# A projection as undivided float32 products instead of three float32r products

## The chip, the core and the metric

The kernel runs on one core of one Trainium2 chip. The metric is the device time of an execution in microseconds (us); the median of three runs is compared. The engines are TensorE (PE in the profile, its loads of the stationary operand PEld), ScalarE (ACT), VectorE (DVE), GpSimd (POOL) and SyncE (SP), which issues the DMAs.

## What is computed

A tower of one block over 64 images of 64 patches with 192 features, in three parts: a token mixer, an attention layer with a memory that is updated token by token, and a feed-forward layer. The change touches the projection of the second part. There, for a normalised row `xn` (192 features) and each of k, q and v:

```python
def _modifier(x, w1, b1, w2, b2):
    h = jax.nn.gelu(x @ w1.T + b1, approximate=False)
    return h @ w2.T + b2
...
k = xn @ Wk.T + 0.1 * _modifier(xn, km_w1, km_b1, km_w2, km_b2)
v = xn @ Wv.T + 0.1 * _modifier(xn, vm_w1, vm_b1, vm_w2, vm_b2)
q = xn @ Wq.T + 0.1 * _modifier(xn, qm_w1, qm_b1, qm_w2, qm_b2)
k = _ln(k.reshape(b, s, H, HD), lnk_g, lnk_b)
...
```

with 12 heads (H) of 64 (HD). All inputs are float32.

## The kernel before

Every engine has its own list of instructions, written out in order in one block (`@block.tensor` and so on); they meet through semaphores (`wait_ge`, `then_inc`, and `need`, which waits where a count is positive). So the order on an engine is the order of the code, and an instruction that waits holds up all behind it on its engine.

**First stage, to 422 us.** A short chain first multiplies the five matrices w0 to w4 into one. Then a pipeline runs over 32 pairs of patches: SP loads three weight matrices and the inputs of a pair (`load_pair`, lines 323 to 334, two buffers), TensorE forms q, k, v and p1 products in chunks (lines 485 to 567), and between the chunks of pair n it does the small products of pairs n-1 (transposes at line 519, scores) and n-2. DVE works in the same steps (line 1242); its line 1262 copies the transposed q and k, its line 1276 forms the sum that TensorE transposes at line 537. The result goes to a scratch tensor in device memory.

**The projection's weights** are prepared within this stage. SP loads them at lines 351 to 357, after it has waited for `bt_copied`, since the tile `cw` lies over the buffer `chain_w[1]` of the matrix chain. `cw` has two slots of 128 partitions and 2304 columns (k, q, v): slot 0 for features 0 to 127, slot 1 (113 rows used, AUG) for features 128 to 191, the 48 hidden values of the modifier and its bias. DVE takes the mean over each head's 64 columns off (`centre_weights`) and splits the result into `cw_hi`, a float32r tile, and `cw_lo`, the rest (`split_weights`). These four blocks follow DVE's own work in steps 2, 3, 4 and 5 (`step_b_and_weights`, line 1302).

**Second stage, from 440 us.** GpSimd fills constants (lines 1084 to 1089), then 32 tiles of 128 rows pass through a pipeline; in step s five to six tiles are in work, tile x = s at the input, t = s - 1 at the projection, j, k, l, m behind. TensorE's list of a step is at lines 789 to 833: it opens with 64x64 products (line 708) and the 12 transposes of `turn_kq` (line 657, 32 times in all, once per tile), and the six pieces of the projection (`project`) lie between other work in the order 1; 3, 0; 2; 4, 5. `PIECES` (line 58) holds their columns, widths (512, 256, 256, 512, 512, 256) and which of k, q, v they belong to. Each piece is the sum over the two slots of `xr_hi*cw_hi + xr_hi*cw_lo + xr_lo*cw_hi`.

The projection's input `x_aug` (four columns of 128: the first 128 features, and three versions of the rest with the GELU values of k, q, v below) is written by ACT (`copy_x`, `gelu`), in one buffer. ACT copies it to `xr_hi` (`high_part`, line 992) and DVE forms `xr_lo` (`low_part`, line 1495), both in two buffers; TensorE waits for `xr_ready` before piece 1 (line 622).

A product is one call of `mm` (line 442) in the code. In the trace a product of float32 operands is two pairs of LDWEIGHTS and MATMUL, one of float32r operands is one pair.

Of the kernel before, what the change touches and what calls it, by code (L numbers as in the profile page):

```python
# [18 lines left out]
F32R = mybir.dt.float32r  # L19
# [48 lines left out]
 mod_mm mod_ready gate_mm gate_ready xr_hi xr_ready  # L68
# [39 lines left out]
def build(nc, d, out):  # L108

    with ExitStack() as ctx:  # L110
# [42 lines left out]
        gate_b = sb("gate_b", [R2 + 1, ATT])  # L153
# [6 lines left out]
        cw_hi = sb("cw_hi", [P, 2, ALL], F32R)  # L160
        cw_lo = sb("cw_lo", [P, 2, ALL], F32R)

# [59 lines left out]
        cw = chain_w[1].rearrange("p a b -> p (a b)").rearrange("p (k n) -> p k n", k=2)  # L222
# [11 lines left out]
        x_aug = part("second", P, 4, P)  # L234
        xg1 = part("second", P, P)
        xg2 = part("second", R2 + 1, P)
# [37 lines left out]
        xr_hi, xr_lo = [[sb(f"{name}{i}", [P, 4, P], F32R) for i in range(2)] for name in ("xr_hi", "xr_lo")]  # L274
# [20 lines left out]
        def _(sp):  # L295
# [55 lines left out]
            sp.wait_ge(S["bt_copied"], 2)  # L351
            settled(sp)
            for dst, src in [(cw[:, 0, :], d["kqvT"][0:P]), (cw[0:R2, 1, :], d["kqvT"][P:ATT]),
                             (cw[R2:AUG, 1, :], d["modT"]), (mod1a[:, :], d["mod1T"][0:P]), (mod1b[:, :], d["mod1T"][P:2 * P]),
                             (gate_a[:, :], d["gateT"][0:P]), (gate_b[:, :], d["gateT"][P:ATT + 1]), (wo[:, :, :], d["WoT"]),
# [85 lines left out]
        def _(pe):  # L441
# [136 lines left out]
            pe.wait_ge(S["cw_ready"], 2)  # L578
# [19 lines left out]
            def modifier(x):  # L598
# [3 lines left out]
                for part, w in enumerate((mod1a, mod1b)):  # L602
                    for i in range(2):
                        last = nc.tensor.matmul(PS[0:MOD_PAIR, 7, i * P:(i + 1) * P], w[:, i * MOD_PAIR:(i + 1) * MOD_PAIR],
                                                x_aug[:, part, :], start=part == 0 and i == 0, stop=part == 1,
                                                skip_group_check=True)
# [231 lines left out]
        def _(act):  # L838
# [50 lines left out]
            act.wait_ge(S["region_ready"], 6)  # L889
# [742 lines left out]
```

## Time and profile before

| | us |
|---|---|
| median of three runs | 1265.63 |
| the three runs | 1265.08, 1265.63, 1268.97 |
| the profiled execution | 1262.91 |
| its span | 1260.7 |
| TensorE busy | 1169.6 (93%), 18596 matmuls |
| loads of the stationary operand busy | 954.3 (76%) |
| DVE, ACT, GpSimd busy | 786.3, 722.8, 560.7 |
| HBM read, written | 154.87 MB, 22.02 MB |

The span is from the first to the last instruction, and the execution's time is 2.2 us more. TensorE's ends are modelled and its instructions overlap, so its busy time says when it had something in work, not how fast it went: the distance between starts tells that.

### The profile page before, as it was taken

Reading aid. Unit: us, or ns where it says so; the run is one execution under the profiler, and the core shown is the slowest. Engines: PE = TensorE matmul, PEld = TensorE weight load, DVE = VectorE, ACT = ScalarE, POOL = GpSimd, SP = SyncE. Lnnn points to the kernel's source line nnn. Section 1 sums busy time; section 2 is a strip of 40 time slices with the busy share of each in tenths; the row PEclk is TensorE's granted clock in tenths of the full one; section 3 lists DMA queues with packets and bytes.
Section 4 is the critical chain, followed back from the end, with each engine's and each line's share of the span. In section 5 each row is a group of like instructions: output and inputs, shape, how many; then the busy total and the mean of one; then the engine's idle time right before and its main releaser. Section 6 shows DMA issues by size and latency. Waiting matters only on the chain.

```text
span 1260.7 us, 47618 instructions
## 1 busy us (share of the span) xinstructions
PE 1169.6 (93%) x18596; PEld 954.3 (76%) x18596; DVE 786.3 (62%) x2152; ACT 722.8 (57%) x1955; POOL 560.7 (44%) x690
## 2 busy tenths in 40 slices
PE   5899999999999558999999999999999999999975
PEld 5865666666666356888888888888888888888864
DVE  0027433333333335787888888887887887888862
ACT  0012222222222247788888888888888888888752
POOL 0000000000000046676776676776676776676631
PEclk8999999999999778999999999999999999999997
DMA  9979999999998001212222222222222222222220
GB/s 320 341 279 352 360 373 375 375 382 372 374 369 330 16 13 25 50 36 41 49 45 39 49 47 39 49 47 41 47 46 39 49 47 40 48 48 36 45 43 21
DMA packets 220196, 179.54 MB, mean 142 GB/s; under 512 B 164406, under 2 KB 190073, under 8 KB 219513
## 3 DMA queue, kind: packets, MB, share of 16 engines
q1 hardware_dynamic: 220010, 176.94, 45.2%
q8 instruction: 131, 2.15, 0.7%
q14 instruction: 55, 0.45, 0.1%
HBM read 154.87 MB, written 22.02 MB: 140 GB/s over the span
## 4 chain that ended last, share of the span: by engine, by line
POOL 36%; PE 31%; issue 23%; DVE 6%; SPq 2%; DMA 1%; ACT 1%; POOLq 0%; DVEq 0%; ACTq 0%
PE PS L443 28%; POOL region L1148 15%; POOL region L1131 6%; POOL region L1136 3%; POOL region L1142 2%; POOL region L1114 1%; POOL region L1098 1%; POOL region L1121 1%; POOL region L1107 1%; DVE region L1454 1%; PE PS L519 1%; SPq L312 1%; POOL region L1111 1%; POOL region L1100 1%; PE PS L537 1%
## 5 line engine op out<-in xcount | busy, mean ns | idle before, releaser
L443 PE MATMUL PS<-region 64*64 64x64 f32 (+6 forms) x5864 | 349.9, 284 | 20.7 <-DVE region L1196 12.2
L443 PEld LDWEIGHTS PS<-region 64*64 64x64 f32 (+3 forms) x5864 | 228.4, 137 | 120.4 <-issue 107.0
L1148 POOL TENSOR_TENSOR region<-region,powers 128x12 f32<-128x12 f32 x96 | 237.2, 2471 | 7.6 <-POOL region L1142 0.2
L1077 POOL TENSOR_TENSOR region<-region,powers 128x1 f32<-128x1 f32 x32 | 6.1, 189 | 404.0 <-DVE region L1256 404.0
L708 PE MATMUL PS<-region 64*64 64x64 f32 x4608 | 154.4, 220 | 2.3 <-ACT region L959 2.1
L708 PEld LDWEIGHTS PS<-region 64*64 64x64 f32 x4608 | 144.4, 134 | 14.9 <-issue 9.2
L443 PE MATMUL PS<-cw_hi,xr_hi 128*128 128x256 f32 (+3 forms) x384 | 145.5, 379 | 3.8 <-DVE xr_lo L1495 1.2
L926 ACT ACTIVATE region<-PS 128x512 f32<-128x512 f32 (+1 forms) x192 | 93.7, 489 | 77.6 <-PE PS L443 74.4
L443 PE MATMUL PS<-cw_lo,xr_hi 128*128 128x256 f32 (+3 forms) x384 | 130.6, 340 | 0.0
L443 PE MATMUL PS<-cw_hi,xr_lo 128*128 128x256 f32 (+3 forms) x384 | 130.4, 340 | 0.0
L849 ACT ACTIVATE region<-PS 128x384 f32<-128x384 f32 x32 | 15.7, 491 | 192.7 <-PE PS L443 192.7
L1131 POOL TENSOR_TENSOR region<-region,powers 128x12 f32<-128x12 f32 x32 | 74.8, 2337 | 107.5 <-DVE region L1448 107.5
L1378 DVE TENSOR_REDUCE region<-region 128x12 f32<-128x768 f32 x96 | 90.2, 943 | 10.5 <-ACT region L931 10.5
L999 ACT ACTIVATE region<-region 128x64 f32<-128x64 f32 x384 | 94.8, 335 | 0.0
L443 PEld LDWEIGHTS PS<-cw_hi,xr_hi 128*128 128x128 f32 (+1 forms) x384 | 73.7, 192 | 16.9 <-ACT region L938 1.8
L906 ACT ACTIVATE region<-PS,vecs 128x256 f32<-128x256 f32 (+1 forms) x128 | 75.9, 670 | 14.0 <-PE PS L657 13.8
L931 ACT ACTIVATE region<-region 128x768 f32<-128x768 f32 x96 | 80.1, 838 | 1.0
L443 PEld LDWEIGHTS PS<-cw_hi,xr_lo 128*128 128x128 f32 (+1 forms) x384 | 73.3, 191 | 8.8
L443 PEld LDWEIGHTS PS<-cw_lo,xr_hi 128*128 128x128 f32 (+1 forms) x384 | 74.5, 194 | 7.1
L443 PE MATMUL PS<-p1w,region 128*128 128x192 f32 x384 | 74.4, 335 | 0.0
L443 PE MATMUL PS<-wo,region 128*128 128x192 f32 x384 | 71.0, 335 | 2.0 <-ACT region L895 2.0
L698 PE MATMUL PS<-region 64*64 64x64 f32 x3072 | 61.3, 226 | 11.3 <-issue 8.4
(171 smaller groups left out, 2184.6 us busy)
## 6 DMA issues: line engine op xcount, KB each, us to landing
region<-in_Wq SPq DMA_DIRECT2D x32, 1152.0 KB, 5.9
region<-in_Wk SPq DMA_DIRECT2D x32, 1152.0 KB, 8.2
region<-in_Wv SPq DMA_DIRECT2D x32, 1152.0 KB, 8.0
region<-in_x SPq DMA_DIRECT2D x32, 384.0 KB, 6.9
n_scratch<-region SPq DMA_DIRECT2D x64, 192.0 KB, 3.5
region<-h_scratch SPq DMA_DIRECT2D x64, 96.0 KB, 3.1
region<-in_w SPq DMA_DIRECT2D x2, 2304.0 KB, 13.4
region<-i_scratch SPq DMA_DIRECT2D x256, 12.0 KB, 1.8
```

What stands on the lines that cost most here:

```text
L443: return nc.tensor.matmul(dst, lhsT, rhs, start=first, stop=last)
L698: done = nc.tensor.matmul(dst(slice(to, to + 64), h), lhsT[rows, h, :], rhs(rows, h), start=h < 2, stop=stop, skip_group_check=True)
L708: done = nc.tensor.matmul(dst(rows, h), eT[rows, h, :], rhs(rows, h), start=start and h == odd, stop=stop, skip_group_check=True)
L906: act.activation(kqT[:, pairs, m, :], PS[:, bank, at:at + n * P].rearrange("p (a b) -> p a b", a=n), ACT.Identity, scale=(lnk_g, lnq_g)[m] ...
L926: act.activation(raw[:, col:col + width], PS[:, PIECE_BANK[i], 0:width], ACT.Copy).then_inc(S["raw_ready"], 1)
L931: act.activation(sq[:, m * KD:(m + 1) * KD], raw[:, m * KD:(m + 1) * KD], ACT.Square, scale=HD ** -0.5).then_inc(S["sq_ready"], 1)
L999: last = act.activation(vs[j % 2][:, h * HD:(h + 1) * HD], raw[:, 2 * KD + h * HD:2 * KD + (h + 1) * HD], ACT.Copy, scale=rs[:, 2 * HEADS ...
L1131: pool.tensor_tensor(norm[:, 1, :], norm[:, 0, :], square_root[:, 0:HEADS], ALU.pow).then_inc(S["n1"], 1)
L1136: pool.tensor_tensor(nscale[:, :, :], mask_n.unsqueeze(1).to_broadcast([P, HEADS, SEQ]), norm[:, 5, :].unsqueeze(2).to_broadcast([P, HEADS ...
L1142: pool.tensor_tensor(rs_var[:, cols], ssq[:, cols], eps[:, cols], ALU.add).then_inc(S["rs_var"], 1)
L1148: pool.tensor_tensor(rs[:, cols], rs_var[:, cols], root[:, cols], ALU.pow).then_inc(S["rs_ready"], 1)
L1378: dve.tensor_reduce(ssq[:, m * HEADS:(m + 1) * HEADS], sq.rearrange("p (g d) -> p g d", d=HD) [:, m * HEADS:(m + 1) * HEADS, :], AX, ALU.a ...
```

## The change

The projection's products take the float32 operands as they are. What goes: the float32r tiles `cw_hi`, `cw_lo`, `xr_hi`, `xr_lo`; the split of the weights on DVE; `high_part` on ACT and `low_part` on DVE; their signals. What comes: `x_aug` in two buffers of its own, written and read by the parity of the tile; `cw` as a tile of its own, so that SP's loads no longer wait for `bt_copied`; rows up to 128 in the second slot of `cw`, in `gate_b` and in `xg2`, zero in the weights; the centring in six blocks, one for each slot and each of k, q, v, in the steps 2 to 7; the memset of the two `x_aug` before GpSimd's wait for the end of the first stage.

```diff
-        cw_hi = sb("cw_hi", [P, 2, ALL], F32R)
-        cw_lo = sb("cw_lo", [P, 2, ALL], F32R)
+        cw = sb("cw", [P, 2, ALL])
...
-        xr_hi, xr_lo = [[sb(f"{name}{i}", [P, 4, P], F32R) for i in range(2)] for name in ("xr_hi", "xr_lo")]
+        x_aug = [sb(f"x_aug{i}", [P, 4, P]) for i in range(2)]
...
             load_pair(Step(0, 1))
-            sp.wait_ge(S["bt_copied"], 2)
-            settled(sp)
             for dst, src in [(cw[:, 0, :], d["kqvT"][0:P]), (cw[0:R2, 1, :], d["kqvT"][P:ATT]),
-                             (cw[R2:AUG, 1, :], d["modT"]), (mod1a[:, :], d["mod1T"][0:P]), (mod1b[:, :], d["mod1T"][P:2 * P]),
+                             (cw[R2:P, 1, :], d["modT"]), (mod1a[:, :], d["mod1T"][0:P]), (mod1b[:, :], d["mod1T"][P:2 * P]),
...
-            pe.wait_ge(S["cw_ready"], 2)
+            pe.wait_ge(S["cw_ready"], 6)
...
                     if i == 1:
-                        pe.wait_ge(S["xr_ready"], t + 1)
                         pe.wait_ge(S["mod_ready"], 3 * t + 3)
...
                     dst = PS[:, PIECE_BANK[i], 0:width]
-                    n = 0
-                    for k, parts in ((0, P), (1, AUG)):
-                        for xs, ws in ((xr_hi[t % 2], cw_hi), (xr_hi[t % 2], cw_lo), (xr_lo[t % 2], cw_hi)):
-                            slot = 0 if k == 0 else 1 + m
-                            last = mm(dst, xs[0:parts, slot, :], ws[0:parts, k, col:col + width], n == 0, n == 5)
-                            n += 1
-                    last.then_inc(S["piece_mm"], 1)
+                    mm(dst, x_aug[t % 2][:, 0, :], cw[:, 0, col:col + width], True, False)
+                    mm(dst, x_aug[t % 2][:, 1 + m, :], cw[:, 1, col:col + width], False, True).then_inc(S["piece_mm"], 1)
...
             def copy_x(x):
                 act.wait_ge(S["xT_mm"], x + 1)
-                need(act, "xr_ready", x)
+                need(act, "piece_mm", 6 * (x - 1))
+                need(act, "mod_mm", x - 1)
                 need(act, "gate_mm", x)
...
+            for buf in x_aug:
+                pool.memset(buf[:, :, :], 1.0).then_inc(S["region_ready"], 1)
             pool.wait_ge(S["h_out0"], PAIRS // 2 * 32)
             pool.wait_ge(S["h_out1"], PAIRS // 2 * 32)
-            for i, (dst, value) in enumerate(((x_aug, 1.0), (xg2, 1.0), (y2T2, 0.0), (dT, 0.0), (inv, 0.0))):
+            for i, (dst, value) in enumerate(((xg2, 1.0), (y2T2, 0.0), (dT, 0.0), (inv, 0.0))):
...
-            dve.wait_ge(S["region_ready"], 5)
+            dve.wait_ge(S["region_ready"], 7)
...
-                if s.known and 2 <= s.n < 6:
-                    (centre_weights, split_weights)[s.n % 2]((s.n - 2) // 2)
+                if s.known and 2 <= s.n < 8:
+                    centre_weights(s.n - 2)
```

The new `centre_weights` of one block:

```python
def centre_weights(part):

    k, m = divmod(part, 3)
    group = cw[:, k, m * KD:(m + 1) * KD].rearrange("p (g d) -> p g d", d=HD)
    mine = slice(m * HEADS, (m + 1) * HEADS)
    if part == 0:
        dve.wait_ge(S["cw_in"], 160)
        dve.tensor_scalar(cw[R2:P, 1, :], cw[R2:P, 1, :], 0.1, None, ALU.mult).then_inc(S["cw_step"], 1)
    ...
```

On TensorE, around piece 2 of a tile in the second stage, between the output projection (`wo`) and the transposes of the next input, there stood before (a row is a product of the program, x6 six in a row; the width is that of the moving operand):

```order
L443 MATMUL PS<-wo,region 128x192 x6
L443 MATMUL PS<-cw_hi,xr_hi 128x256
L443 MATMUL PS<-cw_lo,xr_hi 128x256
L443 MATMUL PS<-cw_hi,xr_lo 128x256
L443 MATMUL PS<-cw_hi,xr_hi 128x256
L443 MATMUL PS<-cw_lo,xr_hi 128x256
L443 MATMUL PS<-cw_hi,xr_lo 128x256
L594 MATMUL PS<-cst,region 128x128
```

and now:

```order
L437 MATMUL PS<-wo,region 128x192 x6
L437 MATMUL PS<-cw,x_aug 128x256 x2
L588 MATMUL PS<-cst,region 128x128
L589 MATMUL PS<-cst,region 64x128
L588 MATMUL PS<-cst,region 128x128
```

Six products of a piece became two; what stands before and behind is the same.

On DVE, in step 2 of the first stage, between the step's last instruction (the scaling of its result) and the first of step 3, there stood before:

```order
L1300 TENSOR_SCALAR region<-region 128x192
L1224 TENSOR_SCALAR region<-region 49x2304
L1226 TENSOR_REDUCE cw_sum<-region 128x36
L1228 TENSOR_SCALAR cw_mean<-cw_sum 128x36
L1230 TENSOR_TENSOR region<-region,cw_mean 128x2304
L1250 SCALAR_TENSOR_TENSOR region<-PS,region 128x192
```

and now:

```order
L1275 TENSOR_SCALAR region<-region 128x192
L1208 TENSOR_SCALAR cw<-cw 64x2304
L1210 TENSOR_REDUCE cw_sum<-cw 128x12
L1212 TENSOR_SCALAR cw_mean<-cw_sum 128x12
L1214 TENSOR_TENSOR cw<-cw,cw_mean 128x768
L1225 SCALAR_TENSOR_TENSOR region<-PS,region 128x192
```

The block now covers a third of a slot's columns; the other blocks follow in the steps behind it.

## Rows read from the trace of the kernel before

In a timeline and in the chain a row gives the start and the length in us, the engine, the line, what was done, and, in square brackets, how long the engine stood idle before it and what ended that. In the busy time by stretch a row gives the stretch, its length, for each of PE, PEld, DVE, ACT and POOL the busy us and in brackets the instructions, then TensorE's granted clock (1.00 is full speed), the DMA engines' share and GB/s. The list of waits gives us in total, how often, and the longest. A group row gives its count, then busy us, mean ns of one, and idle us before.

**Rows 1.** Busy time of the engines in three stretches of the run.

```profile
60.00:420.00 360.00, 353.49 (x2586) 226.85 (x2585) 147.32 (x445) 89.73 (x337) 22.14 (x60) 1.00 0.93 347
...
441.00:516.00 75.00, 53.35 (x688) 45.96 (x688) 39.77 (x99) 44.49 (x105) 41.43 (x51) 0.82 0.14 26
516.00:1179.00 663.00, 656.23 (x13782) 585.37 (x13779) 542.56 (x1449) 546.48 (x1399) 468.31 (x529) 1.00 0.24 44
```

**Rows 2.** Timeline of TensorE: line 657 at five steps of the second stage.

```profile
471.40 2.38 PE L657 MATMUL PS<-cst,region 128*128 128x128 f32 x12 [4.24 <-DVE wo L1317]
...
491.78 2.82 PE L657 MATMUL PS<-cst,region 128*128 128x128 f32 x12 [4.60 <-DVE region L1384]
...
516.13 1.53 PE L657 MATMUL PS<-cst,region 128*128 128x128 f32 x12
...
1178.90 1.72 PE L657 MATMUL PS<-cst,region 128*128 128x128 f32 x12
...
1202.29 1.53 PE L657 MATMUL PS<-cst,region 128*128 128x128 f32 x12
```

**Rows 3.** TensorE's list of waits, 460 to 1240 us, one entry.

```profile
PE PS L698 <- issue: 8.4, 30, 1.2
```

**Rows 4.** Timeline of TensorE, one full step.

```profile
877.76 2.22 PE L443 MATMUL PS<-wo,region 128*128 128x192 f32 x12
...
882.62 0.50 PE L443 MATMUL PS<-cw_hi,xr_hi 128*128 128x512 f32 x1
882.96 0.39 PE L443 MATMUL PS<-cw_lo,xr_hi 128*128 128x512 f32 x1
...
884.13 0.28 PE L443 MATMUL PS<-cw_hi,xr_hi 128*128 128x256 f32 x1
...
884.84 0.60 PE L604 MATMUL PS<-region,mod1a 128*112 128x128 f32 x4
```

**Rows 5.** Timeline of TensorE, first stage, a run of 384-wide products.

```profile
75.66 1.51 PE L443 MATMUL PS<-region 128*64 128x384 f32 x8
```

**Rows 6.** Timelines of TensorE (line 519) and DVE (the weights), first stage.

```profile
97.73 0.64 PE L519 MATMUL PS<-cst,region 128*96 128x128 f32 x4
...
111.77 0.64 PE L519 MATMUL PS<-cst,region 128*96 128x128 f32 x4
...
122.95 0.64 PE L519 MATMUL PS<-cst,region 128*96 128x128 f32 x4
...
135.47 0.64 PE L519 MATMUL PS<-cst,region 128*96 128x128 f32 x4
...
168.78 0.64 PE L519 MATMUL PS<-cst,region 128*96 128x128 f32 x4
...
94.37 1.36 DVE L1224 TENSOR_SCALAR region<-region 49x2304 f32<-49x2304 f32 x1
...
98.56 2.56 DVE L1230 TENSOR_TENSOR region<-region,cw_mean 128x2304 f32<-128x2304 f32 x1
...
109.67 2.56 DVE L1239 TENSOR_TENSOR cw_lo<-region,cw_hi 128x2304 fp32r<-128x2304 f32 x1
```

**Rows 7.** Chain that ended last, in order of time, 436 to 454 us.

```profile
440.31 0.54 POOL region L1087
...
451.87 0.64 ACT xr_hi L992
452.53 0.70 DVE xr_lo L1495
```

**Rows 8.** Timelines of GpSimd and DVE, second tile step.

```profile
466.18 2.27 POOL L1148 TENSOR_TENSOR region<-region,powers 128x12 f32<-128x12 f32 x1
...
467.89 1.83 DVE L1384 TENSOR_TENSOR region<-region 128x768 f32<-128x768 f32 x2
```

**Rows 9.** Groups of weight loads by form: busy us, mean ns of one.

```profile
L443 PEld LDWEIGHTS PS<-cw_hi,xr_lo 128*128 128x128 f32 x192 | 36.7, 191 | 4.5
```

**Rows 10.** Part 4 of the page: chain that ended last, by engine.

```profile
POOL 36%; PE 31%; issue 23%; DVE 6%; SPq 2%; DMA 1%; ACT 1%; POOLq 0%; DVEq 0%; ACTq 0%
```

More of the change, by code:

```diff
@@ L18 @@
 F32 = mybir.dt.float32
-F32R = mybir.dt.float32r
 ALU = mybir.AluOpType
@@ L233, in build @@
         xh = part("second", P, ATT)
-        x_aug = part("second", P, 4, P)
         xg1 = part("second", P, P)
-        xg2 = part("second", R2 + 1, P)
+        xg2 = part("second", P, P)
         gate = [part("second", P, ATT) for _ in range(4)]
@@ L604, in modifier @@
                         last = nc.tensor.matmul(PS[0:MOD_PAIR, 7, i * P:(i + 1) * P], w[:, i * MOD_PAIR:(i + 1) * MOD_PAIR],
-                                                x_aug[:, part, :], start=part == 0 and i == 0, stop=part == 1,
+                                                x_aug[x % 2][:, part, :], start=part == 0 and i == 0, stop=part == 1,
                                                 skip_group_check=True)
@@ L887, in _ @@
             pipeline(act, PAIRS, 2, step_b)
-            act.wait_ge(S["region_ready"], 6)
+            act.wait_ge(S["region_ready"], 7)
             def turned_out(l):
@@ L946, in gelu @@
                 for m, (at, i) in enumerate(((slice(0, MOD), 0), (rows, 0), (rows, 1))):
-                    act.activation(x_aug[rows, 1 + m, :], PS[at, 7, i * P:(i + 1) * P], ACT.Gelu,
+                    act.activation(x_aug[x % 2][rows, 1 + m, :], PS[at, 7, i * P:(i + 1) * P], ACT.Gelu,
                                    bias=mod_bias[at, i:i + 1]).then_inc(S["mod_ready"], 1)
@@ L985, in relu @@
                 act.activation(f1[:, :], PS[:, 6, 2 * P:3 * P], ACT.Relu, bias=ffn_b1).then_inc(S["f1_ready"], 1)
-            def high_part(x):
-                act.wait_ge(S["mod_ready"], 3 * x + 3)
-                act.wait_ge(S["xlin_copied"], 2 * x + 2)
-                need(act, "piece_mm", 6 * (x - 1))
-                need(act, "xr_ready", x - 1)
-                act.activation(xr_hi[x % 2][:, :, :], x_aug[:, :, :], ACT.Copy).then_inc(S["xr_hi"], 1)
             def scale_v(j):
@@ L1233, in split_weights @@
[L1233 to L1240 removed]
+            def centre_weights(part):
[3 more added lines that the diff above has]
+                if part == 0:
+                    dve.wait_ge(S["cw_in"], 160)
+                    dve.tensor_scalar(cw[R2:P, 1, :], cw[R2:P, 1, :], 0.1, None, ALU.mult).then_inc(S["cw_step"], 1)
+                dve.wait_ge(S["cw_step"], 2 * part + 1)
+                dve.tensor_reduce(cw_sum[:, k, mine], group, AX, ALU.add).then_inc(S["cw_step"], 1)
+                dve.wait_ge(S["cw_step"], 2 * part + 2)
+                dve.tensor_scalar(cw_mean[:, k, mine], cw_sum[:, k, mine], 1.0 / HD, None, ALU.mult).then_inc(S["cw_step"], 1)
+                dve.wait_ge(S["cw_step"], 2 * part + 3)
+                dve.tensor_tensor(group, group, cw_mean[:, k, mine].unsqueeze(2).to_broadcast([P, HEADS, HD]),
+                                  ALU.subtract).then_inc(S["cw_ready"], 1)
@@ L1490, in normalise @@
                 dve.tensor_scalar(xh[:, :], xn[:, :], rstd_parts[:, 5:6], None, ALU.mult).then_inc(S["xh_ready"], 1)
-            def low_part(x):
-                dve.wait_ge(S["xr_hi"], x + 1)
-                need(dve, "piece_mm", 6 * (x - 1))
-                dve.tensor_tensor(xr_lo[x % 2][:, :, :], x_aug[:, :, :], xr_hi[x % 2][:, :, :].bitcast(F32), ALU.subtract).then_inc(S["xr_ready"], 1)
             def ffn_out(l):
@@ L1597, in host_layout @@
     d["mod1T"] = tall(np.concatenate([k1, gap(R2 - MOD), q1, gap(R2), v1], axis=1))
-    d["modT"] = np.concatenate([np.concatenate([a[f"attn_{m}m_w2"].T, row(a[f"attn_{m}m_b2"])]) for m in "kqv"], axis=1)
+    below = np.zeros((P - AUG, KD), np.float32)
+    d["modT"] = np.concatenate([np.concatenate([a[f"attn_{m}m_w2"].T, row(a[f"attn_{m}m_b2"]), below]) for m in "kqv"], axis=1)
     d["kqvT"] = np.concatenate([a["attn_Wk"].T, a["attn_Wq"].T, a["attn_Wv"].T], axis=1)
-    d["gateT"] = np.concatenate([a["attn_Wg"].T, row(a["attn_bg"])])
+    d["gateT"] = np.concatenate([a["attn_Wg"].T, row(a["attn_bg"]), np.zeros((2 * P - ATT - 1, ATT), np.float32)])
     d["WoT"] = a["attn_Wo"].T.reshape(HEADS // 2, P, ATT).transpose(1, 0, 2)
```

35 lines of the change are left out of this document (6 added, 29 removed).

## The prediction

> **What bounds the kernel now.** I read the stretches first. From 516 to 1179 us, the stage of the 32 tiles once it is full, TensorE is busy 656.23 of 663 us, DVE 542.56, ACT 546.48, GpSimd 468.31, and the DMA engines a quarter of their time [rows 1]. A busy PE proves little by itself, so the start times come next. The transposes of line 657 open each step. From the one at 516.13 to the one at 1178.90 there are 28 steps, (1178.90 - 516.13) / 28 = 23.67 us each [rows 2]. In that stage the longest entry in TensorE's list of waits is 8.4 us over 30 waits, 0.28 us a step, before line 698, where a chain through DVE has a fixed length [rows 3]. So TensorE works through its list almost without a gap: a microsecond more in its list is a microsecond more in the step. The stage of the 32 pairs before it is the same kind: PE 353.49 of 360 us busy, while the DMA engines stand at 0.93 [rows 1]; its steps, read from the transposes of line 519, are (168.78 - 135.47) / 3 = 11.10 us [rows 6].
>
> **Part 1, the projection's products.** Per tile there are six pieces, three 512 wide and three 256 wide, each with two contraction slots. Before, a slot is three float32r products of one instruction each: 36 instructions. Start to start, five of them at 512 take 884.13 - 882.96 = 1.17 us, 0.234 each; six at 256 take 884.84 - 884.13 = 0.71 us, 0.118 each [rows 4]. That is 18 x 0.234 + 18 x 0.118 = 6.34 us a tile.
> After, a slot is one float32 product, and every float32 product of this kernel is two instructions. No row shows one with 512 columns, so I bound it. The output projection (wo, 192 columns) has 12 instructions in 2.22 us [rows 4]; less the length of the last one (0.33) and what the first one takes extra (0.10), (2.22 - 0.33 - 0.10) / 11 = 0.163 us from start to start, that is 2 x 192 columns at 2.4 GHz (0.160) and 2.5 ns. At 384 columns eight instructions, running two by two on the halves of the array, last 1.51 us, of which the first has some 0.05 extra and the last 0.49 is its own length: (1.51 - 0.49 - 0.05) / 3 = 0.323 a pair [rows 5], again 2 x 384 / 2.4 and 2.5 ns. By this line an instruction at 512 takes 0.429 us and one at 256 takes 0.216. Twelve of each: 5.15 + 2.59 = 7.74 us a tile. In passes: six before, eight after. The first-instruction delay after a group of 64x64 products is 0.34 - 0.23 = 0.11 us for float32r [rows 4] and about 0.10 for float32 at wo, so that cancels.
> Difference: **+1.40 us a tile**. From below the bound is the pure column count, 12 x 0.427 + 12 x 0.213 = 7.68, +1.34. From above: a float32r instruction at 512 takes 0.234 where its columns need 0.213, 9% more; if wide float32 products had the same excess, 7.68 x 1.09 = 8.4, +2.05. I take the line through 192 and 384, since both points are float32 and the excess does not show at either.
> The Trainium skill, FP8 and Floating Point Precision, section Matmul Precision, says that true FP32 is four passes through the array; the 0.163 us for half of a 192-column product agrees, and it adds nothing to the sum.
> Over the 28 full steps: 28 x 1.40 = **+39.2 us**. Nothing hides it, because the neighbours on TensorE are already back to back.
>
> **Part 2, the split of the input.** ACT loses line 992 (0.63 us a tile), DVE loses line 1495 (0.69) [rows 7]. In full steps neither engine is the bound, and the cover is TensorE's own list: worth 0. Once, at the first tile, both lie on the chain of waits: GELU ends at 451.87, then 0.64 and 0.70, then the first piece. After, the first piece follows the GELU: **-1.3 us** [rows 7]. At the second tile the same pair stands before line 1384 on DVE, but its second product also needs GpSimd's power (started 466.18, 2.27 us long, so 468.45), while DVE began the two products at 467.89 (0.9 each); the wait that takes over gives back all but 0.3 [rows 8].
>
> **Part 3, the start of the tile stage.** GpSimd's memset of x_aug, 0.54 us, leaves the chain between the stages; DVE now waits also for the last small memset, about 0.17: **-0.4 us**, if the load of h has landed by then; from 0 to -0.5 [rows 7]. Tiles 0 to 2 run in steps with real waits of TensorE (4.24 before 471.40, 4.60 before 491.78 [rows 2]) and partly at half clock (granted 0.82 over 441 to 516 us [rows 1]). Three tiles at 1.40 are 4.2, half clock adds about 0.5; against it stand the 0.3 of part 2 twice, and waits late in the third step that the longer pieces fill. I take **+2.4**, bounds 0 to 6. The last tile's step (1178.90 to 1202.29 [rows 2], already shorter than a full one) is taken at **+1.2**.
>
> **Part 4, the weights in the first stage.** DVE centres and splits the weights between its pair steps, in four blocks: a scaling and a centring of 6.75 us (94.37 to 98.56 + 2.56), a split of 3.9 (a conversion as long as the scaling, 1.36, and the subtraction of 2.56 that ends at 112.23), and both again for the second slot without the scaling [rows 6]. DVE stands in order, so the block holds up its line 1262 and 1276 of the next step and TensorE behind them. The price is in the steps: 97.73, 111.77, 122.95, 135.47, that is 14.04, 11.18 and 12.52 us where 11.10 is normal, 4.4 us too long together; the 3.9 us block cost 0.1 [rows 6]. After, there are six blocks, one in each of six steps. A reduction and a subtraction over a third of the columns take a third of 2.56 and some 0.1 fixed, 0.95 each, and the small scaling between them 0.2: 2.1 us, the first with 1.36 more, 3.5. All lie under 3.9, so **-4.3 us**; from -4.6 to -2, should loads set the pace when TensorE stops waiting (0.93 of the DMA time is used).
> The ten weight loads on SP no longer wait for bt_copied, and are issued some 12 us earlier. They stand behind the loads of pair 1 in a stretch where the DMA engines are full, and pair 2 waits for TensorE to leave its buffer: 0.
>
> **The sum.** 39.2 + 1.2 + 2.4 - 1.3 - 0.4 - 4.3 = +36.8 us. On the profiled execution's 1262.91 that gives 1299.7. That execution lies 2.7 below the median of the three timed ones, 1265.63; the same difference on the median gives **1302 us**.
>
> **Rivals.**
> *Wide float32 products carry the 9% excess*: 2.05 instead of 1.40 a tile, 31 tiles x 0.65 = +20: 1322. Against: none at 192 or 384 columns. 7%.
> *The weight blocks still hold up DVE*, or loads then set the pace: the 4.3 us do not come back, 1306. 7%.
> *Faster, by weight loads.* Were TensorE paced by its loads of the stationary operand, the count would decide: 36 loads a tile before, 24 after. Place: the pieces of all 32 tiles; price: 12 loads at the 0.11 us at which 128-column transposes follow each other, 1.3 us x 32 = -42, and -6 of parts 2 to 4: 1218. It decides only where a product streams for less than its load takes. For: loads are busy 585.37 of 663 us [rows 1]. Against: loads of 0.19 us at 256 columns follow at 0.118, at 512 columns at 0.234 [rows 4, 9]: the pace goes with the columns streamed. 2%. The Trainium skill, Perfetto Trace Analysis, section Identifying the Most-Contended Engine, says to judge by the busy share of LDWEIGHTS, not of matmuls; by that rule the change would help, and the start times here speak against it.
> *Faster, by the freed engines.* If a loop through ACT and DVE set the 23.67 us, with TensorE only filling it, the step would fall by the 0.63 of line 992 until TensorE's list is longer than the loop: about -20 and -6, which gives 1240. For: the chain that ended last goes through GpSimd for 36% and TensorE for only 31% [rows 10]. Against: TensorE has no gap that another engine ends [rows 3]. 4%.
> *No change*: the eight passes hide in waits that these views do not show, 1263. 3%.
>
> **Chances and range.** The forecast's own case (1302, parts 1 to 4 with their bounds: 1294 to 1310) holds 77%. About 0.3%, 4 us, is what a measurement of this kernel tells from no change. Faster by more 6%, within 3%, slower by more 91%. The range for 8 in 10 takes in the case without part 4 and part of the excess: 1289 to 1318.
>
> **What would show it.** Right: full steps of 25.1 us between the transposes that open them; 512-wide float32 instructions following at 0.43 and 256-wide at 0.22; line 519's steps all near 11.1 from 97 us on; the first piece 0.1 us after the GELU. Wrong: steps at 23.7 or below; wide instructions at 0.47; a new wait of TensorE for ACT or DVE in full steps; first-stage steps that still read 12 to 14 us.

## The result, and the profile after

Timed beside the kernel before on the same chip, the changed kernel takes **1301.16 us** (median of 4 runs, 1299.39 to 1301.68) against 1265.36 (1264.27 to 1268.97). The ratio is 1.0275, with a 95% interval of 1.0253 to 1.0298: slower, by 35.8 us. The profiled execution has a span of 1299.5 us; that of the kernel before, from which the rows ahead of the prediction come, has 1260.7.

First the busy time by stretch in the changed kernel, with the columns of [rows 1].

```profile
60.00:420.00 360.00, 356.89 (x2600) 229.85 (x2598) 142.49 (x456) 90.20 (x339) 22.13 (x60) 1.00 0.93 348
506.00:1200.00 694.00, 687.06 (x13285) 545.57 (x13281) 520.41 (x1402) 522.59 (x1344) 450.75 (x521) 1.00 0.23 42
```

TensorE is as full as before in both stages, with fewer instructions in the second (13285 in 694 us for 13782 in 663) and about as many in the first (2600 for 2586); DVE and ACT have become a little emptier, since the split is gone and the step is longer. Next the transposes that open a full step (line 657 before, line 645 now), which answer to [rows 2].

```profile
512.40 1.53 PE L645 MATMUL PS<-cst,region 128*128 128x128 f32 x12
...
1215.65 1.53 PE L645 MATMUL PS<-cst,region 128*128 128x128 f32 x12
1239.76 1.53 PE L645 MATMUL PS<-cst,region 128*128 128x128 f32 x12
```

The 28 steps take (1215.65 - 512.40) / 28 = 25.12 us each; before it was 23.67. Most steps of after are 25.05 us and most of before 23.63, a difference of 1.42. The first full step opens 3.7 us earlier than before (512.40 for 516.13). So the loss is made between these two marks, nearly all of it as a fixed price for each step.

What TensorE does in one of these steps, from its timeline, which answers to [rows 4]:

```profile
901.55 2.85 PE L437 MATMUL PS<-cw,x_aug 128*128 128x512 f32 x8
904.24 0.60 PE L598 MATMUL PS<-x_aug,mod1a 128*112 128x128 f32 x4
...
907.54 0.93 PE L686 MATMUL PS<-region 64*64 64x64 f32 x48 [0.22 <-issue]
...
923.65 1.03 PE L437 MATMUL PS<-cw,x_aug 128*128 128x256 f32 x4
924.52 0.27 PE L588 MATMUL PS<-cst,region 128*128 128x128 f32 x1
```

Two instructions make one float32 product. The four of the last piece take 924.52 - 923.65 = 0.87 us, 0.217 each at 256 columns. The eight at 901.55 are four at 512 and four at 256 columns, and take 904.24 - 901.55 = 2.69 us; less 0.87 and 0.10 for the start behind a group of 64x64 products, (2.69 - 0.97) / 4 = 0.430 each at 512. The one gap in the step is the old one ahead of across(), still 0.22 us. TensorE's list of waits from 506 to 1200 us says the same, as in [rows 3]:

```profile
PE PS L686 <- issue: 7.6, 28, 1.2
...
PE PS L696 <- issue: 0.5, 2, 0.3
```

Over 28 full steps these two lines are all the waits of TensorE that the profile lists.

In the first stage, line 519 is now line 513, and DVE's weight blocks are thirds. Its starts answer to [rows 6]:

```profile
99.37 0.64 PE L513 MATMUL PS<-cst,region 128*96 128x128 f32 x4
...
110.44 0.64 PE L513 MATMUL PS<-cst,region 128*96 128x128 f32 x4
...
121.50 0.64 PE L513 MATMUL PS<-cst,region 128*96 128x128 f32 x4
...
418.77 0.60 PE L513 MATMUL PS<-cst,region 128*96 128x128 f32 x4
```

The steps are 11.07 and 11.06 us where they were 14.04, 11.18 and 12.52, and all further ones are 11.07 but the last (9.53, in both kernels). DVE's timeline with the first block:

```profile
96.00 1.36 DVE L1208 TENSOR_SCALAR cw<-cw 64x2304 f32<-64x2304 f32 x1
97.40 0.95 DVE L1210 TENSOR_REDUCE cw_sum<-cw 128x12 f32<-128x768 f32 x1
98.38 0.17 DVE L1212 TENSOR_SCALAR cw_mean<-cw_sum 128x12 f32<-128x12 f32 x1
98.59 0.96 DVE L1214 TENSOR_TENSOR cw<-cw,cw_mean 128x768 f32<-128x768 f32 x1
```

From 96.00 to 99.55 it is 3.55 us, the other five are 2.1.

### The profile page after: what moved, and what is told of

The parts are those of the page before. It is cut to its first block, busy times and chain, and to the rows that moved or that the text cites. A ratio compares the mean times of both kernels' runs of the same rounds, so it can differ in the third digit from the quotient of the medians.

```text
span 1299.5 us, 46700 instructions
## 1 busy us (share of the span) xinstructions
PE 1216.8 (94%) x18212; PEld 918.9 (71%) x18212; DVE 763.0 (59%) x2128; ACT 704.4 (54%) x1923; POOL 550.1 (42%) x691
## 3 DMA queue, kind: packets, MB, share of 16 engines
HBM read 155.06 MB, written 22.02 MB: 136 GB/s over the span
## 4 chain that ended last, share of the span: by engine, by line
POOL 33%; PE 31%; issue 26%; DVE 5%; DMA 2%; SPq 2%; ACT 0%; POOLq 0%; DVEq 0%; ACTq 0%
PE PS L437 28%; POOL region L1131 14%; POOL region L1114 6%; POOL region L1119 2%; POOL region L1125 1%; PE PS L513 1%; POOL region L1081 1%; POOL region L1090 1%; POOL region L1104 1%; SPq L308 1%; POOL region L1097 1%; DVE region L1429 1%; POOL region L1094 1%; POOL region L1083 1%; PE PS L531 1%
## 5 line engine op out<-in xcount | busy, mean ns | idle before, releaser
L437 PE MATMUL PS<-cw,x_aug 128*128 128x256 f32 (+1 forms) x768 | 276.3, 496 | 1.5 <-ACT region L914 0.7
L437 PEld LDWEIGHTS PS<-cw,x_aug 128*128 128x128 f32 x768 | 138.4, 191 | 89.3 <-issue 76.1
L696 PEld LDWEIGHTS PS<-region 64*64 64x64 f32 x4608 | 146.2, 136 | 15.3 <-issue 9.7
L686 PEld LDWEIGHTS PS<-region 64*64 64x64 f32 x3072 | 53.3, 138 | 21.4 <-issue 21.1
L437 PEld LDWEIGHTS PS<-p1w,region 128*128 128x128 f32 x384 | 60.8, 190 | 9.6 <-issue 8.9
L1359 DVE TENSOR_TENSOR region<-region 128x768 f32<-128x768 f32 x64 | 61.3, 957 | 5.2 <-POOL region L1131 2.8
L437 PEld LDWEIGHTS PS<-wo,region 128*128 128x128 f32 x384 | 62.3, 192 | 2.7 <-ACT region L883 2.2
```

Of the source, the lines that this page charges most:

```text
L437: return nc.tensor.matmul(dst, lhsT, rhs, start=first, stop=last)
L686: done = nc.tensor.matmul(dst(slice(to, to + 64), h), lhsT[rows, h, :], rhs(rows, h), start=h < 2, stop=stop, skip_group_check=True)
L696: done = nc.tensor.matmul(dst(rows, h), eT[rows, h, :], rhs(rows, h), start=start and h == odd, stop=stop, skip_group_check=True)
L1359: dve.tensor_tensor(kq[:, m * KD:(m + 1) * KD].rearrange("p (g d) -> p g d", d=HD), raw[:, m * KD:(m + 1) * KD].rearrange("p (g d) -> p g ...
```

## The experiments

Each runs beside the kernel before; the ratios are to it. A version of the changed kernel is compared with its 1301.2 us, and its opening transposes have line numbers of their own.

**The freed engines: do ScalarE and VectorE's instructions count?** To the changed kernel the copy and the subtraction are given back, with TensorE waiting for them.

```
+ act.activation(xr_hi[x % 2][:, :, :], x_aug[x % 2][:, :, :], ACT.Copy)
+ dve.tensor_tensor(xr_lo[x % 2][:, :, :], x_aug[x % 2][:, :, :], xr_hi[x % 2][:, :, :].bitcast(F32), ALU.subtract)
+ pe.wait_ge(S["xr_ready"], t + 1)
```

> The changed kernel, with ACT's float32r copy of the input (128x512) and DVE's subtraction put back, and TensorE's first piece waiting for them as before; the projection doesn't use their results. Theory (TensorE's own list sets the step, the other engines have time to spare): full steps stay at 25.05 us, and only the first tile pays the pair's 1.3 us, so about 1302.5 us against 1301.2 for the changed kernel. Rival (a loop through ACT and DVE sets the step, and their freed time is worth something): the step grows by up to 0.63 us, 28 x 0.63 = 18 us, 1319 us.

Measured: 1303.21 us (1302.57 to 1304.79), ratio 1.0295 (1.0277 to 1.0313). TensorE's waits in 506 to 1200 us:

```profile
PE PS L689 <- issue: 7.6, 28, 1.2
```

The same 7.6 us as without them. So the two instructions cost nothing in full steps, which shows part 2 of the prediction, and rules out that the freed engines would have paid.

**The weight blocks.** The six centring blocks of the changed kernel, joined into two, in steps 2 and 4:

```
- if s.known and 2 <= s.n < 8:
-     centre_weights(s.n - 2)
+ if s.known and s.n in (2, 4):
+     for part in range(3):
+         centre_weights(3 * (s.n // 2 - 1) + part)
```

> The changed kernel, with the centring of the weights in two blocks (three parts each, in steps 2 and 4) instead of six. The blocks are 1.36 + 3 x 2.1 = 7.7 us and 6.3 us long. Theory (a block on DVE longer than some 3.9 us holds TensorE up by what it is longer, as 6.75 us cost 2.9 us in the kernel before): +3.8 and +2.4 in the first stage, 1307.5 us; the steps of the first stage after them read 14.9 and 13.5 instead of 11.07. Rival (the gain in the first stage came from elsewhere, the earlier weight loads or the missing split): no difference, 1301 us.

Measured: 1309.12 us (1306.00 to 1310.58), ratio 1.0331 (1.0308 to 1.0355). The starts of line 513, TensorE's two waits inside the first of these steps, and the stretch behind them:

```profile
99.30 0.64 PE L513 MATMUL PS<-cst,region 128*96 128x128 f32 x4
...
105.39 0.52 PE L437 MATMUL PS<-region 96*64 96x64 f32 x8 [2.71 <-DVE region L1237]
106.78 0.45 PE L531 MATMUL PS<-cst,region 128*96 128x128 f32 x1 [0.87 <-DVE region L1251]
...
116.89 0.64 PE L513 MATMUL PS<-cst,region 128*96 128x128 f32 x4
```

```profile
105.39:116.90 11.51, 10.64 (x62) 6.96 (x62) 3.41 (x13) 2.44 (x10) 0.29 (x2) 0.70 0.78 276
```

The step with the 7.6 us block is 17.59 us, the one with the 6.2 us block 13.43 (expected 14.9 and 13.5). The first is 2.7 us longer than expected because, behind 3.6 us of waits, TensorE was granted 0.70 of full speed from 105.39 to 116.90 us, part of that time the lower of its two levels. So a wait of TensorE cost its own length and then some.

The other way round, the kernel before with nothing changed but its weights' centring and split in six blocks of a third:

```
- if s.known and 2 <= s.n < 6:
-     (centre_weights, split_weights)[s.n % 2]((s.n - 2) // 2)
+ if s.known and 2 <= s.n < 8:
+     prepare_weights(s.n - 2)
```

> The kernel before, float32r products and all, only with the preparation of the weights (centring and split) in six blocks of a third of a slot each, in steps 2 to 7, instead of four. Blocks are 3.6 us, the first 4.9 us. Theory (the length of one block decides, not the work in all): of the 4.4 us that the first stage loses, all but about 1 us comes back, 1262 us against 1265.4. Rival (what the first stage gained is the split that is gone, or the earlier loads): no difference, 1265.4 us.

Measured: 1261.47 us (1258.15 to 1263.67), ratio 0.9960 (0.9945 to 0.9975). Its first block (scaling, centring and split of a third) is long enough to make one step 12.45 us; all others are 11.07. From the first transposes of line 519 to the last it gains 3.2 us. Its profiled execution has the same span as that of the kernel before, 1260.7 us, because TensorE's first 48 products and the end took longer in it (both are taken up below); the gain shows in these steps and in the medians. These two runs show part 4: the gain is that of smaller blocks, it has nothing to do with float32, and the kernel before can have it too.

**What the second slot costs.** The changed kernel with the first slot alone.

```
- mm(dst, x_aug[t % 2][:, 0, :], cw[:, 0, col:col + width], True, False)
- mm(dst, x_aug[t % 2][:, 1 + m, :], cw[:, 1, col:col + width], False, True)
+ mm(dst, x_aug[t % 2][:, 0, :], cw[:, 0, col:col + width], True, True)
```

> The changed kernel without the products of the second contraction slot in the projection (features 128 to 191 and the modifier are left out of k, q and v); all else stays. It takes 6 x 0.429 + 6 x 0.216 = 3.87 us a tile off TensorE's list. Theory (TensorE sets the step as long as it is full): if it still does at the shorter list, full steps of 25.05 - 3.87 = 21.2 us and some 1301 - 31 x 3.87 = 1181 us. Rival (another loop lies close below 25 us): the steps stop where that loop is, between 21.2 and 25.05, and TensorE shows a new wait in each full step that names it; with a loop at 23 us about 1240 us.

Measured: 1215.03 us (1212.51 to 1216.50), ratio 0.9593 (0.9572 to 0.9615). The commonest step is 22.02 us (22.19 in the mean of 28), 3.03 less than 25.05, where the products left out are 3.87. TensorE's waits from 506 to 1129 us, the full steps, tell where the rest went:

```profile
PE PS L685 <- issue: 16.9, 28, 0.9
PE PS L761 <- DVE region L1393: 8.7, 27, 0.9
```

That is 0.60 and 0.32 us for each, where the changed kernel has 0.27 and nothing: 0.65 us of new idle time. From start to start, which also counts what the profile doesn't list as idle, a step of 22.02 us beside one of 25.05 has 3.85 us less in the products, 0.42 more ahead of across() and 0.39 more ahead of the transposes at line 761: 3.85 - 0.81 = 3.04. So the 3.87 is right, and TensorE's list sets the step only down to about a microsecond below the changed kernel's. What waits there is turn_y2() (line 761), for a normalisation on DVE that itself waits for GpSimd's powers.

**A loop, or waits on top of the list?** At this point I held that a loop of the three engines takes 22.0 us whatever TensorE does. Two versions of the kernel before with thirds change TensorE's list further.

```
- for xs, ws in ((xr_hi[t % 2], cw_hi), (xr_hi[t % 2], cw_lo), (xr_lo[t % 2], cw_hi)):
+ for xs, ws in ((xr_hi[t % 2], cw_hi), (xr_hi[t % 2], cw_lo)):       (two products)
+ for xs, ws in ((xr_hi[t % 2], cw_hi),):                             (one product)
```

> The kernel before with its weights prepared in thirds (the version that took 1261.5 us), and of the three float32r products of a slot the one of the input's low part left out: two products, weights high and low, the input rounded to float32r; VectorE's subtraction is gone with it. So the input's low part is left out of the result. TensorE has 2.11 us less to do in each full step (a third of 6.34), which by its list alone makes the step 23.63 - 2.11 = 21.52 us. In the version with one slot the list was 20.9 us and the step 22.02, the rest being TensorE's waits. Theory: these waits belong to a loop of the three engines that takes 22.0 us, so the step is 22.0 to 22.2 us, and the kernel 1261.5 - 28 x 1.55 = 1218 us. Rival: the waits stand behind products whatever the list's length and come on top of it: 21.52 + 1.1 = 22.6 us, 1233 us. Without such waits it would be 1202 us.

Measured: 1220.46 us (1217.26 to 1225.03), ratio 0.9632 (0.9610 to 0.9654), the commonest step 22.2 us (22.38 in the mean).

> The same with one float32r product for each slot; the low parts of the weights and of the input are left out of the result. TensorE's products of the first projection are 2.11 us in a step instead of 6.34, its list some 19.4 us. Theory of the 22.0 us loop: the step stays at 22.0 us (21.8 to 22.2), the same as with two products, total within 5 us of it, 1213 to 1218 us. Rival, waits that come on top of the list: 19.4 + 1.1 = 20.5 us, 1174 us.

Measured: 1214.17 us (1208.92 to 1216.60), ratio 0.9570 (0.9545 to 0.9595). Its steps, and two waits of TensorE that no version so far had:

```profile
816.76 1.53 PE L657 MATMUL PS<-cst,region 128*128 128x128 f32 x12
...
838.39 1.53 PE L657 MATMUL PS<-cst,region 128*128 128x128 f32 x12
```

```profile
PE PS L443 <- ACT region L941: 21.4, 28, 0.8
...
PE PS L443 <- ACT region L912: 10.6, 29, 0.4
```

The commonest step is 21.63 to 21.65 us (22.19 in the mean), with the products 2.11 us shorter than with two. The list is not the bound here, and the sum of list and waits (20.5) is not either. The version with two products also speaks on the loads: it has 24 product instructions and 24 weight loads in a tile, as the changed kernel has, and takes 22.2 us a step instead of 25.05. The pace goes by columns streamed, not by loads.

**Is GpSimd in that loop?** Three additions of epsilon are taken from GpSimd in the version with one product.

```
- pool.tensor_tensor(rs_var[:, cols], ssq[:, cols], eps[:, cols], ALU.add)
- pool.tensor_tensor(rs[:, cols], rs_var[:, cols], root[:, cols], ALU.pow)
+ pool.tensor_tensor(rs[:, cols], ssq[:, cols], root[:, cols], ALU.pow)
```

> The version with one float32r product for each slot, whose step no longer goes by TensorE's list but stays at 21.6 us at least, with GpSimd's instructions in its chain all along. Here the three additions of epsilon ahead of the powers of the head sums are left out on GpSimd (so epsilon is left out of these, and the low parts of input and weights as before): 3 x (0.21 us and 0.07 us to the power behind it) = 0.84 us less on GpSimd in each step. Theory, a loop through GpSimd's own order: the step becomes 20.8 to 21.3 us (some of the 0.84 goes into the waits that GpSimd has between the powers), the kernel 1192 to 1206 us instead of 1214. Rival, the loop does not pass there: step and time stay, 1214 us.

Measured: 1208.16 us (1205.42 to 1215.06), ratio 0.9565 (0.9530 to 0.9600), which overlaps the 0.9570 of the version with them.

```profile
810.62 1.53 PE L657 MATMUL PS<-cst,region 128*128 128x128 f32 x12
...
832.26 1.53 PE L657 MATMUL PS<-cst,region 128*128 128x128 f32 x12
```

Most steps are 21.64 us as before, so my theory fell: the chain of waits had run through these instructions, and 0.84 us less in them did not shorten the step. Fewer steps were longer than that (mean 21.93 for 22.19), and the median is 6.0 us lower, which is within the scatter of the two (1205.42 to 1215.06 and 1208.92 to 1216.60); 0.84 us in each of 28 steps would have been 23.5. The other direction, one more power on GpSimd ahead of the key lengths' powers, in both kernels:

```
+ pool.tensor_tensor(spare[:, :], norm[:, 0, :], square_root[:, 0:HEADS], ALU.pow)
  pool.tensor_tensor(norm[:, 1, :], norm[:, 0, :], square_root[:, 0:HEADS], ALU.pow)
```

> The changed kernel with one more power of 128x12 (2.34 us) on GpSimd in each step, ahead of the powers of the key lengths, its result unused. Theory: TensorE's list of 25.05 us sets the step and the loop of the three engines would take 22.0 + 2.3 = 24.3 us, still less: 1301 to 1302 us, step 25.05 us. Rival, in which the loop has no such room: up to 28 x 2.3 = 64 us more, 1365 us.

> The kernel before with the same additional power on GpSimd. Theory: the loop of 22.0 us and the 2.3 us make 24.3 us, more than the 23.63 us of TensorE's list, so the step becomes 24.3 us (24.2 to 24.6) and the kernel 1266 + 28 x 0.7 = 1286 us. Rival: TensorE's list still sets the step, 1266 us.

Measured: 1349.58 us (1346.77 to 1350.37), ratio 1.0657 (1.0630 to 1.0683), for the changed kernel, and 1338.04 us (1332.05 to 1342.01), ratio 1.0563 (1.0521 to 1.0605), for the kernel before. Two opening transposes of the first:

```profile
837.18 1.53 PE L646 MATMUL PS<-cst,region 128*128 128x128 f32 x12
...
863.66 1.53 PE L646 MATMUL PS<-cst,region 128*128 128x128 f32 x12
```

They are 26.48 us apart; most steps are 26.42. Two of the second:

```profile
834.40 1.53 PE L658 MATMUL PS<-cst,region 128*128 128x128 f32 x12
...
860.03 1.53 PE L658 MATMUL PS<-cst,region 128*128 128x128 f32 x12
```

Here the theory of a 22.0 us loop fell altogether: it gave 25.05 and 24.3, and the steps are 26.42 and 25.63. TensorE's waits from 510 to 1135 us, of the changed kernel with the power, then of the kernel before with it:

```profile
PE PS L687 <- issue: 18.3, 24, 3.3
...
PE PS L763 <- DVE region L1397: 16.3, 23, 0.7
```

```profile
PE PS L775 <- DVE region L1422: 32.3, 24, 1.6
...
PE PS L699 <- issue: 18.5, 24, 3.5
```

In both they are the same two places as with one slot: the transposes of y2, and across(). So what limits is no loop with a length of its own. It is a **path beside TensorE's list**, out of a product of TensorE (the key lengths), through DVE and GpSimd's power, back to TensorE's transposes of y2. It needs some time; what TensorE has to do between the two ends either covers it or doesn't. Of the added 2.34 us the changed kernel took 2.34 - 1.37 = 0.97 us without getting longer, the kernel before 2.34 - 2.00 = 0.34 us. The change made this cover larger, since some of its longer products lie between the ends. The one slot took away cover. The new theory makes a prediction of its own, a power short enough for the room:

```
+ pool.tensor_tensor(spare[:, 0:1], norm[:, 0, 0:1], square_root[:, 0:1], ALU.pow)
```

> The changed kernel with an additional power of one column (0.55 us and its gap) on GpSimd ahead of the powers of the key lengths, where the power of 12 columns (2.34 us) made each step 1.37 us longer (26.42 for 25.05) and in the kernel before 2.00 us (25.63 for 23.63). Theory: from the products of the key lengths to the transposes of y2 runs a path through VectorE and GpSimd beside TensorE's own list, with 2.34 - 1.37 = 0.97 us of room in the changed kernel and 0.34 us in the one before; 0.6 us fit into it: step 25.05 us, 1301 us. Rival: every microsecond there costs something (GpSimd's order at other places): 0.6 x 1.37 / 2.34 = 0.35 us for each step, 1311 us.

Measured: 1301.70 us (1301.57 to 1301.80), ratio 1.0272 (1.0243 to 1.0300), most steps 25.05 us.

```profile
822.88 0.61 POOL L1116 TENSOR_TENSOR spare<-region,powers 128x1 f32<-128x1 f32 x1 [4.23 <-DVE region L1426]
```

0.6 us cost nothing, where a cost in proportion would have given 1311: there is room, and it has an end.

**The path, from start to start.** The starts show the path more directly than the sums of waits. The first transpose of y2 follows the products of the key lengths (64x1) in the changed kernel and with one slot so:

```profile
695.23 0.88 PE L437 MATMUL PS<-cst,region 64*64 64x1 f32 x48
...
704.60 0.27 PE L762 MATMUL PS<-cst,region 128*128 128x128 f32 x1
```

```profile
711.06 0.88 PE L437 MATMUL PS<-cst,region 64*64 64x1 f32 x48
...
719.08 0.33 PE L761 MATMUL PS<-cst,region 128*128 128x128 f32 x1 [0.17 <-DVE region L1393]
```

The median of this distance over the full steps, in all versions that bear on it:

| version | us | what sets it |
|---|---|---|
| changed; changed with the short power | 9.37 | TensorE's list |
| before | 8.75 | TensorE's list |
| one slot; two products; one product; one product without epsilon; the float32r version at the end of this section | 8.02 | the path |
| changed with the power | 10.26 | the path |
| before with the power | 10.27 | the path |

So the path takes 8.02 us, and 2.25 more with the power of 2.34 in it. Its room is 9.37 - 8.02 = 1.35 us in the changed kernel and 0.73 in the kernel before. The 0.62 between them is what pieces 2, 4 and 5 have grown by, the only changed products between the two ends: two of 256 columns and one of 512, 2 x 0.16 + 0.32 = 0.64 us. The added power made the distance 0.89 and 1.52 us longer. The other 0.48 us of each step, in both kernels, lies ahead of across(), where the wait grew from some 0.24 us to 0.76 and 0.77; what makes it grow isn't shown. So the 0.97 and 0.34 us above are what the power left unpaid at both places together, and the room of the path alone is larger. With one slot pieces 2, 4 and 5 lose 1.7 us between the ends, more than the room, and the path shows.

**The early loads.** The wait ahead of the ten weight loads put back into the changed kernel.

```
+ sp.wait_ge(S["bt_copied"], 2)
+ settled(sp)
```

> The changed kernel with the wait ahead of the ten weight loads put back, so that they are issued at some 50 us again instead of at 33. The loads' early issue was priced at nothing: 1301 us, 1300 to 1303, first full step starting at 512 us as in the changed kernel. Rival: the early loads cost the 1.6 us that TensorE's first 48 products took longer at 67.5 us (7.73 us against 6.04), then 1299.5 us and these products back at 6.04 us, the granted clock 1.00 in that stretch; or they gained some 2 us in the start, then 1303 us or more.

Measured: 1298.55 us (1297.66 to 1303.93), ratio 1.0259 (1.0235 to 1.0283), which overlaps the changed kernel's 1.0275. TensorE's first 48 products, in the kernel before, in the changed one, and in this one:

```profile
67.54 6.04 PE L443 MATMUL PS<-region 128*64 128x384 f32 x48 [2.47 <-DVE ffn_bias L1214]
```

```profile
67.49 7.73 PE L437 MATMUL PS<-region 128*64 128x384 f32 x48 [2.48 <-DVE ffn_bias L1197]
```

```profile
66.21 7.74 PE L439 MATMUL PS<-region 128*64 128x384 f32 x48 [2.47 <-DVE ffn_bias L1199]
```

The early loads are worth nothing that these runs can measure: the four runs without them lie on both sides of the changed kernel's median. And they did not slow these products.

**A version that beats both.** The changed kernel's structure (thirds, two input buffers, no copy) with one float32r product for a slot; ScalarE writes the input rounded, DVE's centring writes the weights rounded.

```
- x_aug = [sb(f"x_aug{i}", [P, 4, P]) for i in range(2)]
+ x_aug = [sb(f"x_aug{i}", [P, 4, P], F32R) for i in range(2)]
+ cw_r = sb("cw_r", [P, 2, ALL], F32R)
- mm(dst, x_aug[t % 2][:, 0, :], cw[:, 0, col:col + width], True, False)
+ mm(dst, x_aug[t % 2][:, 0, :], cw_r[:, 0, col:col + width], True, False)
```

> The changed kernel with one float32r product for each slot in place of the float32 one: the input is written rounded by ScalarE itself and the weights by their centring, so there is neither ScalarE's copy of the input (0.63 us in a step) nor a split of the weights (the low parts are left out of the result, as in the version with one product built from the kernel before, 1214 us). Theory: the step there is no longer TensorE's list but a chain through ScalarE and the banks, and the copy stood in ScalarE's slack (it waits 0.55 us for TensorE right behind it), so the step stays at 21.6 us and the kernel at 1210 to 1215 us. Rival: ScalarE's whole list, 541 of 625 us busy, sets the step: 21.0 us, 1195 us.

Measured: **1204.32 us** (1203.18 to 1207.22), ratio 0.9511 (0.9486 to 0.9537). The commonest step is 21.64 us, as I expected; the time is below my range. Its span (1202.0) is 11.5 us under that of the version with one product built from the kernel before (1213.5): 4 us of it are gained before the first full step (502.45 for 506.23), 5 in the 28 steps (22.02 us in the mean for 22.19), the rest behind them. So ScalarE's list isn't the bound; which chain makes the 21.64 us is **open**. It stayed the same with GpSimd's additions taken away, and with ScalarE's copy taken away. TensorE's waits for ScalarE (21.4 us over 28 and 10.6 over 29, above) are new in the versions with one product, and are where I would look next. This version gives up the low parts of input and weights. Among the versions that keep all parts, the kernel before with thirds is the fastest, 1261.47 us.

## Why the prediction was right, point by point

**What bounds the kernel.** Right. TensorE has no new wait in full steps, and the step became longer by exactly what its list did.

**Part 1.** Predicted 0.429 and 0.216 us for an instruction at 512 and 256 columns, measured 0.430 and 0.217; predicted +1.40 a step, measured +1.42; over the 28 steps +39.2 predicted, 703.25 - 662.77 = +40.5 measured. Of the missing 1.3 us, 0.6 are the 1.42 for 1.40; the rest are single steps of 25.1 to 25.6 us, of which the changed kernel has more than the kernel before. The line through the 192- and the 384-column products held at 512; the 9% excess of float32r did not appear, so the rival of 1322 us is out.

**Part 2.** Worth 0 in full steps, as the version with the copies shows. At the first tile -1.3 was predicted. From the first transpose of x to the first piece it was 453.28 - 446.11 = 7.17 us before and 450.12 - 444.34 = 5.78 after, -1.4.

**Part 3.** Mixed. The memset was to give 0.4 us. It gave 0.1: the chain that ended last goes, in the changed kernel,

```profile
436.56 1.99 DMA h_scratch<-region
...
438.61 2.09 DMA region<-h_scratch
...
440.79 0.37 DVE region L1451
```

From the landing of the stored h to DVE it is 440.79 - 438.55 = 2.24 us. Before it was 442.56 - 440.20 = 2.36, over the memsets. The load of h, which the prediction made a condition, had not landed: it took the memset's place. Then tiles 0 to 2: from the first transpose of x to the first full step it was 516.13 - 446.11 = 70.02 us and is 512.40 - 444.34 = 68.06, -2.0, where +2.4 - 1.3 = +1.1 was predicted. That term was mis-sized, by 3 us. The prediction had the longer pieces add 4.2, the clock 0.5, and the waits give back 4.2 + 0.5 - 1.1 = 3.6. The waits were about right: behind the first transpose they add up to 12.6 us, where they were 16.6, so 4.0 came back. What is left is -2.0 - 4.2 + 4.0 = -2.2 us, where the clock was to cost 0.5. The granted clock over the stretch was 0.91, before it was 0.84; that this makes up the 2.2 is likely, and not shown by a run of its own. The last step became 0.72 us longer, for 1.2.

**Part 4.** Predicted -4.3. From the first transposes of the first stage to the last it was 421.78 - 77.10 = 344.68 us and is 418.77 - 78.74 = 340.03, **-4.65**. Loads did not set the pace instead. Early loads: 0, as predicted.

**What the sum left out.** Three stretches moved that the change does not touch. TensorE's 48 products at 67.5 us took 1.7 us longer. The way from the last opening transposes of the first stage to the first of the second grew from 446.11 - 421.78 = 24.33 to 444.34 - 418.77 = 25.57 us, and the end, from the last opening transposes, from 58.4 to 59.7 us. For the first and the last these runs show no tie to the change. The same products take 6.04 us in four and 7.73 or 7.74 us in ten of the fourteen kernels that ran here, with the change and without it. The end is 58.4 us in the kernel before and 61.1 in the kernel before with thirds, which have the same code there. In the middle one, four products of TensorE on the path took 1.65 us instead of 0.92, at a lower granted clock:

```profile
423.36 1.65 PE L437 MATMUL PS<-weff,region 96*128 96x192 f32 x4 [0.71 <-ACT region L845]
```

That is 0.7 of its 1.2 us, and again no property of the change that these runs can show. With all terms: +1.6 - 4.65 + 1.2 - 2.0 + 40.5 + 0.7 + 1.3 = +38.7, which is 1299.5 - 1260.7 up to rounding. The medians differ by 35.8 and the prediction said 36.8. Errors of 1 to 3 us with both signs cancelled, so the match to a microsecond is partly luck; that of the large term is not.

**The rivals.** The faster one by weight loads is out twice: the loads fell by a third, from 36 to 24 a tile, and the kernel got slower; and with 24 loads of either kind the step is 22.2 or 25.05 us. The Trainium skill (Perfetto Trace Analysis, section Identifying the Most-Contended Engine) says to judge TensorE's distance from its limit by the rate of its arithmetic (MFU) and by the busy share of LDWEIGHTS. Taken alone, the second would have misled here: it fell from 585.37 of 663 us [rows 1] to 545.57 of 694, as if TensorE had room, while its list sets the step in both kernels. The one by a loop of the freed engines is out by the version with the copies.

## What to carry to other kernels

Price a change of product type in instructions times columns, from start-to-start times in the same trace, and check first that nothing but TensorE's own list ends its waits; then the price is paid in full. Three float32r products pass a slot's columns three times, one undivided float32 product four times: the split made by hand is the cheaper one as long as the other engines have time for it. A long block on an in-order engine is better cut so that each piece fits into the slack of one step. When a chain of waits runs through an engine, that doesn't make it the bound: add a known cost to it and take one away, since the two may answer differently. And measure a path beside a full engine from start to start between its two ends, once where it is covered and once where it is not: the difference is its room.

## What the runs showed of the hardware

- A float32 product of this kernel is two instructions, each of 0.430 us at 512 columns and 0.217 at 256, that is twice the columns at 2.4 GHz and some 3 to 4 ns; float32r is one of 0.234 and 0.118 [rows 4]. The excess over the columns' time is much smaller for float32.
- Behind a wait of 2.47 us TensorE ran its next 48 products in 6.04 us in one profiled execution and in 7.73 in another. Granted clock over 65 to 75 us, before and after:

```profile
65.00:75.00 10.00, 7.53 (x58) 5.42 (x58) 2.04 (x7) 0.49 (x1) 0.00 (x0) 1.00 0.25 72
```

```profile
65.00:75.00 10.00, 7.53 (x49) 4.66 (x48) 2.04 (x7) 0.49 (x1) 0.00 (x0) 0.83 0.10 14
```

  The same code and the same wait stand there in all fourteen kernels that ran; four (the kernel before, with and without the power, the changed one with the short power, the one without epsilon) took 6.04 us, the other ten 7.73 or 7.74. What decides between the two isn't known from these runs; it moves a single profile by 1.7 us.
- An added instruction of 2.34 us on GpSimd cost 2.00 us in each step of the kernel before and 1.37 in the changed one, though GpSimd had been busy for only 71% and 65% of the time there: room is a matter of the path, not of the busy share. The path through it took 8.02 us in five versions of different length, and 10.26 and 10.27 with the instruction.
